# Order of the seven Strassen-like products in two pairs of a LoRA update kernel

## What is computed

```python
x: (64, 64, 1024)     itok: (64,) in 0..15     cond_weights: (16, 64, 64)
W = cond_weights[itok]
y = einsum('bct,bcd->bdt', x, W)                          # 64 small matrix products
base  = einsum('bsi,oi->bso', y, W_org)                   # 1024 x 1024
q     = einsum('bi,ki->bk', y.mean(axis=1), Wq)
coeffs = softmax(einsum('bk,ek->be', q, lora_keys) / sqrt(128))   # 8 experts
h     = einsum('bsi,eir->bser', y, lora_down)             # rank 64 each, 512 in all
delta = einsum('be,bser,ero->bso', coeffs, h, lora_up)
out   = x + base + delta
```

## Time and profile before

| | us |
|---|---|
| median of 3 runs | 729.07 (729.03 to 729.25) |
| time of the profiled run | 729.7 |
| span of the profiled execution | 727.9 |
| TensorE busy in it | 705.4 (97%) |
| VectorE busy | 489.1 (67%) |
| ScalarE busy | 242.4 (33%) |

### The profile page before, as it was taken

The page is one execution under the profiler, slowest core; times in us unless marked ns, Lnnn a source line. Parts: engine busy times, 40 slices in busy tenths (PEclk is TensorE's granted clock), DMA queues, the critical chain, the costliest instruction groups (busy, mean ns, idle before and its releaser), DMA issues.

```text
span 727.9 us, 10648 instructions
## 1 busy us (share of the span) xinstructions
PE 705.4 (97%) x3385; PEld 591.9 (81%) x3385; DVE 489.1 (67%) x808; ACT 242.4 (33%) x466; POOL 121.3 (17%) x110
## 2 busy tenths in 40 slices
PE   5988999999999999999999999999999999999996
PEld 5776888888888888888887877888888888888885
DVE  2988476575575673664656798676767777676763
ACT  4455245244253361441532732112222222221120
POOL 1600000000000000000000023332233332233332
PEclk9999999999999999999999999999999999999999
DMA  9975475583673753532452746667676667666643
GB/s 260 287 244 156 135 230 186 169 249 118 200 228 114 231 175 112 160 135 59 145 173 77 267 167 188 216 229 231 232 231 231 220 228 227 226 203 223 213 136 104
DMA packets 101034, 138.61 MB, mean 190 GB/s; under 512 B 18794, under 2 KB 70002, under 8 KB 98290
## 3 DMA queue, kind: packets, MB, share of 16 engines
q1 hardware_dynamic: 100480, 137.82, 59.2%
q10 hardware_dynamic: 498, 0.10, 0.1%
HBM read 82.32 MB, written 55.57 MB: 189 GB/s over the span
## 4 chain that ended last, share of the span: by engine, by line
PE 86%; DVE 5%; issue 3%; DMA 2%; SPq 1%; ACT 1%; POOL 1%; POOLq 0%; DVEq 0%; ACTq 0%
PE x_ps L1297 22%; PE w_ps L1297 16%; PE x_ps L1234 11%; PE h_ps L1200 11%; PE x_ps L1200 10%; PE w_ps L1234 8%; PE y_ps L1177 6%; DMA down_raw<-in_L_ffn_lora_down_dram 1%; PE w_ps L1285 1%; DVE tu_l L760 1%; DVE tb_l L760 1%; DMA blkx<-in_x_dram 1%; POOL blk L495 1%; DVE ysum L775 1%; DVE up_raw L760 1%
## 5 line engine op out<-in xcount | busy, mean ns | idle before, releaser
L495 POOL TENSOR_TENSOR blk<-blk,blkx 128x512 f32<-128x512 f32 x64 | 98.0, 1532 | 294.7 <-DVE blk L763 219.8
L763 DVE TENSOR_TENSOR blk<-w_ps,blk 128x512 f32<-128x512 f32 x96 | 66.0, 688 | 79.9 <-PE w_ps L1234 38.8
L1297 PE MATMUL x_ps<-tb_h,ba_h 128*128 128x512 f32 x256 | 100.0, 390 | 1.3 <-DVE blk L763 0.8
L1297 PE MATMUL x_ps<-tb_l,ba_h 128*128 128x512 f32 x256 | 99.6, 389 | 0.0
L1297 PE MATMUL x_ps<-tb_h,ba_l 128*128 128x512 f32 x256 | 99.6, 389 | 0.0
L526 ACT ACTIVATE ba_h<-bs 128x512 fp32r<-128x512 f32 x64 | 38.0, 626 | 124.3 <-DVE bs L760 124.3
L1297 PE MATMUL w_ps<-tb_h,ba_h 128*128 128x512 f32 x192 | 74.9, 390 | 0.0
L1297 PE MATMUL w_ps<-tb_l,ba_h 128*128 128x512 f32 x192 | 74.7, 389 | 0.0
L1297 PE MATMUL w_ps<-tb_h,ba_l 128*128 128x512 f32 x192 | 74.7, 389 | 0.0
L763 DVE TENSOR_TENSOR blk<-x_ps,blk 128x512 f32<-128x512 f32 x64 | 42.5, 683 | 39.4 <-PE x_ps L1297 39.4
L775 DVE TENSOR_REDUCE ysum<-y_full 128x8 f32<-128x512 f32 x64 | 41.6, 680 | 36.2 <-ACT y_full L526 36.2
(11 more groups left out here) (96 smaller groups left out, 1372.3 us busy)
## 6 DMA issues: line engine op xcount, KB each, us to landing
x_sb<-in_x_dram SPq DMA_DIRECT2D x32, 512.0 KB, 4.3
y_dram<-y_full SPq DMA_DIRECT2D x64, 256.0 KB, 3.0
yb<-y_dram SPq DMA_DIRECT2D x32, 512.0 KB, 7.4
blkx<-in_x_dram SPq DMA_DIRECT2D x32, 512.0 KB, 7.0
out_dram<-blk SPq DMA_DIRECT2D x64, 256.0 KB, 3.9
r_dram<-blk SPq DMA_DIRECT2D x56, 256.0 KB, 2.3
blk<-r_dram SPq DMA_DIRECT2D x14, 1024.0 KB, 6.8
t_dram<-st SPq DMA_DIRECT2D x16, 448.0 KB, 3.8
```

The costliest lines, as they stand in the source:

```text
L495: pool.tensor_tensor(blk[p % 3][:, b, :], blk[p % 3][:, b, :], blkx[:, h, n, :], ALU.add).then_inc(x_added, 1)
L763: nc.vector.tensor_tensor(dst, a, b, ALU.add).then_inc(done, 1)
L1297: mm = nc.tensor.matmul(bank, ba[s][n][:, k, :], tb[w][n][:, k, :], start=(first and k == 0 and i == 0), stop=(k == 3 and i == 2), skip_gr ...
```

## The change

No instruction is added or removed, and no operand changes. The calls are put in another order on three engines.

On TensorE the fourteen products of a quarter go from

P1 P2 P6 P7 P5 (j0), P1 (j1), P3 P4 (j0), P6 P2 P5 P7 P3 P4 (j1)

to

P1 P7 P2 P6 (j0), P1 (j1), P5 (j0), P6 (j1), P3 P4 (j0), P2 P5 P7 P3 P4 (j1).

The wait for `w_copied` and `t_sum` goes from P2 to P7, which is now the first on `w_ps`. ACT and DVE get their splits, sums and copies in an order to match, and the `split_y` and `sum_y` calls move later.

```diff
@@ scalar: the up stage
                 take_r(j0, 0, P1, r1_ready)
-                if more:
-                    split_y(n + 6)
                 hi_block(j1, P1, 0, 0)
                 hi_sum(j0, P3, 3)
+                hi_block(j0, P4, 1, 1)
                 if q == 0:
                     split_up(P4, 4)
                 take_r(j0, 2, P6, r2_ready)
-                hi_block(j0, P4, 1, 1)
+                hi_sum(j1, P6, 1)
+                take_r(j1, 0, P1, r1_ready)
+                hi_block(j1, P2, 0, 1)
                 take_r(j0, 3, P5, r4_ready)
...
+                hi_sum(j1, P7, 2)
+                if more:
+                    split_y(n + 6)
...
@@ vector: the up stage
                 lo_sum(j0, P5, 0)
-                if more:
-                    sum_y(n + 6)
-                    sum_y(n + 7)
-                end_c11(j0)
-                lo_sum(j0, P3, 3)
+                lo_block(j1, P1, 0, 0)
                 if q == 0:
                     dve.wait_ge(tu_sum, 3)
                     sub(U21, U21, U22, tu_sum)
-                    split_up(P4, 7)
-                lo_block(j1, P1, 0, 0)
-                if more:
-                    if q == 0:
-                        split_y(n)
-                        split_y(n + 2)
-                        split_y(n + 4)
-                    split_y(n + 6)
+                end_c11(j0)
                 sum_1(j1)
                 sum_2(j1)
+                lo_sum(j0, P3, 3)
+                if q == 0:
+                    split_up(P4, 7)
+                lo_sum(j1, P6, 1)
+                if more:
+                    sum_y(n + 6)
+                    sum_y(n + 7)
                 lo_block(j0, P4, 1, 1)
+                sum_4(j1)
                 end_c22(j0)
...
@@ tensor
             def up_2(j):
                 if j >= 1:
                     pe.wait_ge(c11_ready, j)
-                if j >= 2 and j % 2 == 0:
-
-                    pe.wait_ge(w_copied, 4 * min(j // 2, 4))
-                    pe.wait_ge(t_sum, 8 * min(j // 2, 4) - 2)
                 up_product(j, P2, w_ps[:, 0, :], True, 3)
...
             def up_7(j):
                 if j >= 1:
                     pe.wait_ge(c21_ready, j)
+                if j >= 2 and j % 2 == 0:
+
+                    pe.wait_ge(w_copied, 4 * min(j // 2, 4))
+                    pe.wait_ge(t_sum, 8 * min(j // 2, 4) - 2)
                 up_product(j, P7, w_ps[:, 1, :], True, 6)
...
                 up_1(j0)
+                up_7(j0)
                 up_2(j0)
                 up_6(j0)
-                up_7(j0)
+                up_1(j1)
                 up_5(j0)
-                up_1(j1)
+                up_6(j1)
                 up_3(j0)
                 up_4(j0)
-                up_6(j1)
                 up_2(j1)
```

More of the change, by code:

```diff
@@ L703, in _ @@
                 take_r(j0, 2, P6, r2_ready)
-                hi_block(j0, P4, 1, 1)
+                hi_sum(j1, P6, 1)
+                take_r(j1, 0, P1, r1_ready)
+                hi_block(j1, P2, 0, 1)
                 take_r(j0, 3, P5, r4_ready)
-                hi_sum(j1, P6, 1)
-                hi_block(j1, P2, 0, 1)
-                take_r(j1, 0, P1, r1_ready)
                 hi_sum(j1, P5, 0)
+                take_r(j1, 2, P6, r2_ready)
+                hi_sum(j1, P7, 2)
+                if more:
+                    split_y(n + 6)
+                else:
+                    split_t(P6, slice(0, 2))
                 take_r(j0, 1, P3, c12_ready)
+                hi_sum(j1, P3, 3)
                 if more:
                     split_y(n + 1)
-                hi_sum(j1, P7, 2)
+                hi_block(j1, P4, 1, 1)
                 if more:
                     split_y(n + 3)
[L716 to L720, removed]
-                if more:
-                    split_y(n + 5)
                 else:
@@ L726, in _ @@
                 if more:
-                    split_y(n + 7)
+                    split_y(n + 5)
                 else:
@@ L1080, in _ @@
                 lo_sum(j0, P5, 0)
+                lo_block(j1, P1, 0, 0)
+                if q == 0:
+                    dve.wait_ge(tu_sum, 3)
+                    sub(U21, U21, U22, tu_sum)
+                end_c11(j0)
+                sum_1(j1)
+                sum_2(j1)
+                lo_sum(j0, P3, 3)
+                if q == 0:
+                    split_up(P4, 7)
+                lo_sum(j1, P6, 1)
                 if more:
@@ L1083, in _ @@
                     sum_y(n + 7)
-                end_c11(j0)
-                lo_sum(j0, P3, 3)
+                lo_block(j0, P4, 1, 1)
+                sum_4(j1)
+                end_c22(j0)
                 if q == 0:
-                    dve.wait_ge(tu_sum, 3)
-                    sub(U21, U21, U22, tu_sum)
-                    split_up(P4, 7)
-                lo_block(j1, P1, 0, 0)
+                    split_y(n)
+                lo_block(j1, P2, 0, 1)
+                lo_sum(j1, P5, 0)
+                if q == 0:
+                    split_y(n + 2)
+                    split_y(n + 4)
+                lo_sum(j1, P7, 2)
                 if more:
-                    if q == 0:
-                        split_y(n)
-                        split_y(n + 2)
-                        split_y(n + 4)
                     split_y(n + 6)
[L1097 to L1103, removed]
+                else:
+                    split_t(P6, 3, slice(0, 2))
                 end_c21(j0)
-                lo_sum(j1, P5, 0)
+                lo_sum(j1, P3, 3)
                 if more:
                     split_y(n + 1)
-                lo_sum(j1, P7, 2)
+                lo_block(j1, P4, 1, 1)
                 if more:
@@ L1111, in _ @@
                 else:
-                    split_t(P6, 3, slice(0, 2))
+                    split_t(P6, 4, slice(2, 4))
                 end_c11(j1)
[L1114 to L1117, removed]
                 end_c22(j1)
```

1 line of the change is left out of this document (added).

## The result

The changed kernel takes 723.89 us (median of 4 runs, 723.74 to 724.69) beside 729.16 us (729.03 to 729.51) for the kernel before on the same chip. The ratio is 0.9932, with a 95% interval of 0.992 to 0.9945. In a later group of runs on another chip the same two gave 723.95 and 729.02, ratio 0.9927 (0.9915 to 0.994). The forecast was 723.6, in a range of 722.8 to 725.8.

What follows compares the result with a forecast made beforehand. TensorE, busy 97% of the span, was taken as the bound, with only its idle or slow time recoverable. Gains of 4.4 us (first quarter) and 1.1 (last), middle 0, took 729.07 to 723.6 us, range 722.8 to 725.8.

Steps and rivals of the forecast that it cites:

- P6 of the second pair: First quarter: this product, wanted at 61.36, gets its low part from DVE at 61.46, so 0.2 us is lost.
- (d): First quarter's up stage: the remaining 0.36 us of the 6.58 too many, put down to 0.09 per restart and rounding.
- (a): First quarter, before P2: TensorE idles 2.55 us; P7 in second place fills 1.36, leaving 1.19.
- (b): First quarter, before P5: start 1.96 us late behind ACT's copy; an earlier DVE subtraction leaves 0.34.
- (c): First quarter, 61.54 to 65.29: nine slow matmuls cost 1.71 us over normal pace, counted as gone with smaller holes.
- by a hair: First quarter, new order: DVE just not the bound, freeing P4(j1) at 71.3 while TensorE arrives at 71.2.
- DVE in one piece: First quarter: DVE works 14.0 us without a break from 56.47 to the start of `end_c22(j1)`, which ends at 71.2.
- the first quarter gives nothing: Rival: DVE becomes the first quarter's bound, so only the last quarter's 1.1 us stays: 728.0 us, chance 0.06.
- The middle: Six middle quarters: nothing to win and no new wait, up stages staying at 19.05 us; cost 0.
- the slower rival: Second pair's P6 late in each middle quarter behind DVE and ACT queues; 732.6 us if 2.5 late; chance 0.04.
- The last quarter: Last quarter's up stage: P7 fills the 1.07 us before P2, and the base stage follows earlier; gain 1.1 us.
- The rival that the clock falls all the same: First quarter: TensorE still idles twice, so the slow clock stays, costing 1.7 us: 725.3 us, chance 0.12.

## Why the prediction was right, and where not

**The time and its size.** 723.6 was forecast, 723.89 measured; a span 5.5 shorter, measured 5.0. The 0.5 arose in the first quarter: the next stage was to start at 77.03 - 4.4 = 72.63 and started at 73.15. P5 came only 0.05 later than laid out, but P6 of the second pair 0.4 later (61.97 for 61.56), which is the missed wait below; the last 0.1 is pace and restarts. In my term (d), 0.16 of the 0.36 was no loss of time at all: the chain's 77.03 lies that much behind the start of the stage's first matmul.

**(a), the hole before P2: right.** Left was to be 1.19, and P7 to fill 1.36. P2 started at 55.62, P1 and P7 take 0.09 + 2.72 from 51.77: 1.04 left, of which the timeline's 0.88 is what lies behind the modelled end of the matmul ahead. P7 moved to third place brings back the wait of 2.1.

**(b), the copy before P5: right in its mechanism.** `tu_h` was laid out at 58.32 and the copy behind it at 59.28. The timeline of ACT, beside the earlier trace rows, has 58.37 and 59.34:

```profile
58.37 1.06 ACT L526 ACTIVATE tu_h<-up_raw 128x1024 fp32r<-128x1024 f32 x1 [1.03 <-DVE up_raw L760]
59.34 0.58 ACT L526 ACTIVATE blk<-x_ps 128x512 f32<-128x512 f32 x1
61.32 0.60 ACT L526 ACTIVATE blk<-x_ps 128x512 f32<-128x512 f32 x1 [1.10 <-DVE tu_l L760]
```

P5 starts at 59.97 (forecast 59.92). Moving the subtraction alone gained 1.66 in the trace (with the clock up); moving it back lost 1.2 to 1.6 at full clock.

**P6 of the second pair: a wait I had missed.** It was to lose 0.2 for its low part. It lost 0.5 (61.97 where the pace would have given 61.46), for the third row above: ACT's copy after P1 of the second pair, which overwrites `blk` where the raw blocks of `lora_up` had lain, and so waits for the low part `tu_l` of P4's operand (DVE, 59.98 + 1.22 = 61.20). A buffer read by another queue was the step I left out.

**(c), the slow matmuls: the step that failed.** 1.71 us were booked to them, at a granted clock of 0.50, as if all of it lay on the path, and the sum has them gone because the holes get smaller. No run shows a gain of 1.7 from the clock, nor that the size of a hole decides whether it falls. With the three holes filled the clock was 1.00 in every window from 34 to 66 us, with a mean of 0.998 or more in all eleven runs, and that gained 0.41 in the trace and nothing in the median. The other 1.3 of that term was DVE's queue: four splits and a late `end_c22`, beside which TensorE's slow matmuls happened to lie. The 1.7 is there only when both are out of the way: from P5 to P4 it is 5.81 us before, 5.35 with the clock up, and 4.24 with the clock up and the splits moved. I had read each engine's loss by itself and put the whole overhead on TensorE's side. That the sum came out all the same is in part luck: nothing in my sum had booked a gain to DVE's queue, and the change also moves that queue, the subtraction forward (1.66 in the trace) and the splits and sums behind. I had called the latter not the bound "by a hair", which is right of the order after, but did not say that it *was* the bound before. How the remaining 1.1 of the 2.7 from P2 on falls to splits, sums and TensorE's order is not told apart: the two runs on the splits turned up a wait of their own.

**The clock from run to run: I weighed it wrongly.** One trace had nine slow matmuls, and since the three times of before lay within 0.22 us I took them for a part of every execution. They are not: in the fourteen profiles the lower clock came after the wait at 35 to 37 us in five profiles, after the wait near 60 in two, after P2's hole in one, and not at all in six. The spread said nothing, since the price is covered or nearly so, by the wait before P2 when the clock falls near 40 us and by DVE's queue when it falls near 61: of 69 runs of the kernel before, the 32 with a mean clock below 0.9975 average 729.18 us, the 25 above 0.9985 average 729.23. Where less covers it, a fall shows: 1.5 us between the two kinds in the kernel with the subtraction moved back (five runs).

**DVE in one piece: right.** From the low part before `up_raw` it was to work 14.0 us without a pause to `end_c22(j1)`, at 70.5. The timeline of DVE, beside the earlier trace rows:

```profile
57.12 1.21 DVE L760 TENSOR_TENSOR up_raw<-up_raw 128x1024 f32<-128x1024 f32 x1
...
69.90 1.28 DVE L763 TENSOR_TENSOR blk<-w_ps,blk 128x512 f32<-128x512 f32 x2
73.18 0.69 DVE L763 TENSOR_TENSOR blk<-w_ps,blk 128x512 f32<-128x512 f32 x1 [2.00 <-PE w_ps L1236]
```

The second of the two additions merged at 69.90 is `end_c22(j1)`; it ends at 71.18 (forecast 71.2), and P4(j1), at 71.62, doesn't wait. The last row is the addition after P4(j1). So the rival "the first quarter gives nothing" fell, on the point named for it.

**The middle and the slower rival: right.** No wait came up, 19.06 us a stage. The chance of a late copy or low part was not idle: with P7 moved alone there is such a wait in every quarter, and the kernel is slower by 0.9%. It comes between P6 and P5, a pair on one bank that my list of the tight places did not hold; in the full change P1 of the second pair stands between the two.

**The last quarter: right.** 1.1 forecast, 1.11 measured, and with P7 in third place the wait of 0.8 comes back.

**The rival that the clock falls all the same.** Both profiles of the changed kernel have a granted clock of 1.00 in the first up stage, and no run of the nine has a mean below 0.998, where the profiles with a slow stretch have 0.996 or 0.997. The holes of 0.9 and 0.3 were not followed by a slow stretch; those of 1.8 to 2.5 were, in part of the profiles. That the smaller holes are why isn't shown, since after a hole of 3.04, with P7 moved alone, the clock stayed up too.

## What to carry to other kernels

A slow or idle stretch of one engine was worth only what the other engines' queues left of it, here 0.4 of 1.7 us: before booking one, read on each of them when the next hand-over would be ready at the earliest, and count only up to there. Before a product is moved, see whether it parts two that share an accumulation bank: with P7 gone from between P6 and P5, P5 waited 0.69 us for the copy and a quarter took 0.98 longer, so that a part of the reordering tried alone cost more (6.2 us) than the whole brings (5.3). When a copy is moved, look at the buffer that it overwrites too, and at who still reads it (0.35 us before P6 of the second pair).

## What the runs showed of the hardware

In eight of the fourteen profiles the granted clock fell to 0.50 once ahead of the last ten microseconds, for a stretch of some eight or nine matmuls at 0.43 us from start to start instead of 0.23, after waits of TensorE between 1.79 and 2.49 us. It was so in some executions of one program and not in others: the mean clock of the 69 runs of the kernel before goes from 0.996 to 1.000, and those of the two kinds of the kernel with the subtraction moved back are 0.997 and 0.999 or more. The length of the wait alone doesn't decide it: none came after waits of 1.79 (to 36.93 us) and 2.38 (before P2) in the kernel before, of 1.76 before P5 with the splits moved, and of 2.50 and 3.04 in the kernel with P7 moved alone. In the two profiles of the changed kernel none came after the waits of 0.88 and 0.82 us before P2 and of 0.35 before P6. Nor did it always begin at the wait's end: in the kernel with the subtraction moved back five matmuls ran at full pace (61.01 to 62.28) before the slow ones.

In the changed kernel the hole before P2, 0.88 and 0.82 us in its two profiles, hides when TensorE reaches P1 (51.77 and 50.90 us), but P2 itself stands where DVE puts it: in its two profiles at 55.62 and 54.70 us, the next stages at 73.15 and 72.21, the spans 722.9 and 722.0. The first four runs spread over 0.95 us and the later five over 0.4; with the filler at the scores and the same hole five runs spread over 1.4. The order without that hole and without a filler has the widest spread, 3.0 us in six runs, around nearly the same median. That the missing hole is the reason is not shown by so few runs.
